# All eight PSUM banks from one table, re-planned step orders, and the late weight loads moved to another queue

## What is computed

```python
x = _layernorm(x + attn0(x))   # 16 heads of 8, low-rank q and k, causal softmax
x = _layernorm(x + ffn0(x))    # silu gate to 512, two 512x512 layers with gelu, down to 128
x = _layernorm(x + attn1(x))   # 16 heads of 8, softmax without a mask
x = _layernorm(x + ffn1(x))    # router picks 1 of 8 low-rank additions, relu, down to 128
```

## Time and profile before

| | us |
|---|---|
| median of three runs | 955.86 (951.77 to 958.83) |
| the profiled execution, its own time | 957.05 |
| its span, first to last instruction | 955.1 |
| PE busy | 887.5 (93%) |
| DVE busy | 673.9 (71%) |
| ACT busy | 487.8 (51%) |

### The profile page before, as it was taken

One profiled execution on the slowest core, in us unless ns is written; L12 is line 12 of the kernel. 1 busy time (PEld: TensorE's weight loads), 2 busy tenths in 40 slices (PEclk: granted clock), 3 DMA queues, 4 the chain that ended last, 5 costly groups with the idle time before them and its releaser, 6 DMA issues.

```text
span 955.1 us, 19245 instructions
## 1 busy us (share of the span) xinstructions
PE 887.5 (93%) x7076; PEld 690.3 (72%) x7076; DVE 673.9 (71%) x2379; ACT 487.8 (51%) x951; POOL 184.3 (19%) x389
## 2 busy tenths in 40 slices
PE   4598999999999999999999999999999999999995
PEld 3365887867667876678777887788767887778653
DVE  3867657759996569963698579956888659554843
ACT  0043654367455645644647365636555575563461
POOL 1032312003310233100420033101420123011011
PEclk9578999999998999989999999999999999999897
DMA  8514031402232024200243024120422022001200
GB/s 284 144 30 128 14 96 51 114 22 79 69 91 63 1 85 130 84 2 24 69 125 91 8 73 126 55 57 16 125 80 69 7 69 68 1 28 47 84 8 12
DMA packets 48900, 65.17 MB, mean 68 GB/s; under 512 B 5608, under 2 KB 42728, under 8 KB 44232
## 3 DMA queue, kind: packets, MB, share of 16 engines
q1 hardware_dynamic: 46840, 60.38, 21.8%
q10 hardware_dynamic: 1968, 3.57, 1.1%
HBM read 48.46 MB, written 14.68 MB: 66 GB/s over the span
## 4 chain that ended last, share of the span: by engine, by line
PE 47%; DVE 15%; issue 7%; DMA 4%; ACT 2%; SPq 2%; POOL 1%; POOLq 0%; DVEq 0%; ACTq 0%
PE ps_g L981 16%; PE ps_g L912 6%; PE ps_s L894 6%; DVE top L682 5%; PE ps_s L861 4%; PE ps_g L963 3%; PE ps_g L1030 3%; DMA krow<-scratch 2%; PE ps_g L816 1%; ACT prob L556 1%; PE ps_g L1011 1%; PE ps_g L1012 1%; DVE x L752 1%; DMA qrow<-tsplit 1%; PE ps_g L942 1%
## 5 line engine op out<-in xcount | busy, mean ns | idle before, releaser
L556 ACT ACTIVATE prob<-ps_s 128x384 f32<-128x384 f32 (+1 forms) x512 | 250.8, 552 | 111.3 <-PE ps_s L894 86.8
L682 DVE TENSOR_REDUCE top<-ps_s 128x2 f32<-128x512 f32 (+1 forms) x280 | 180.7, 683 | 46.3 <-PE ps_s L861 37.7
L673 DVE CUSTOM_DVE_ANT_0 ps_s<-ps_s,above 128x128 f32<-128x128 f32 x448 | 145.8, 386 | 30.0 <-PE ps_s L861 26.4
L894 PE MATMUL ps_s<-qrow,krow 75*128 75x256 bf16 (+1 forms) x1024 | 159.8, 266 | 7.2 <-DMA qrow<-tsplit 4.4
L861 PE MATMUL ps_s<-krow,qrow 72*128 72x256 bf16 x768 | 146.1, 281 | 13.2 <-DVE top L682 5.7
L493 POOL TENSOR_TENSOR ln_rstd<-ln_var,minus_half 128x2 f32<-128x2 f32 x64 | 45.0, 705 | 419.1 <-DVE ln_var L742 418.9
L894 PEld LDWEIGHTS ps_s<-qrow,krow 75*128 75x128 bf16 x1024 | 89.2, 100 | 47.8 <-ACT prob L556 18.9
L912 PE MATMUL ps_g<-prob,v 128*32 128x256 f32 (+1 forms) x2048 | 121.1, 363 | 1.8 <-DVE glu L763 0.7
L981 PE MATMUL ps_g<-glu,wh 128*128 128x256 f32 x512 | 120.8, 391 | 0.0
L981 PE MATMUL ps_g<-hid,wh 128*128 128x256 f32 x512 | 115.7, 380 | 0.0
L981 PEld LDWEIGHTS ps_g<-glu,wh 128*128 128x128 f32 x512 | 97.8, 196 | 14.7 <-issue 0.8
(11 more groups left out here) (99 smaller groups left out, 1171.6 us busy)
## 6 DMA issues: line engine op xcount, KB each, us to landing
qrow<-scratch SPq DMA_DIRECT2D x30, 576.0 KB
krow<-scratch SPq DMA_DIRECT2D x90, 192.0 KB
scratch<-split SPq DMA_DIRECT2D x96, 128.0 KB, 1.9
wh<-in_wh SPq DMA_DIRECT2D x1, 2048.0 KB, 11.5
xt<-in_xt SPq DMA_DIRECT2D x16, 128.0 KB, 2.4
x<-in_x SPq DMA_DIRECT2D x16, 128.0 KB, 2.3
out<-xout SPq DMA_DIRECT2D x16, 128.0 KB, 2.0
qrow<-tsplit SPq DMA_DIRECT2D x90, 8.0 KB
```

Of the source, the lines that this page charges most:

```text
L556: nc.scalar.activation(prob[s][:, j % 2, g, 0:wide], ps_s2[:, (GROUP * j + g) % PSUM2, 0:wide], ACT.Exp, scale=1.0 / float(np.sqrt(np.floa ...
L673: done = nc.vector.tensor_tensor_reduce(out=bank[:, g * wide:(g + 1) * wide], in0=bank[:, g * wide:(g + 1) * wide], in1=above[:, 2 * P - w ...
L682: nc.vector.tensor_reduce(out=dst, in_=src, axis=AX, op=ALU.max, negate=True).then_inc(maxed[s], 1)
L894: done = nc.tensor.matmul(bank[:, kb * SEQ:(kb + 1) * SEQ - q0], krow[s][n % DEEP[s]][0:ROWSM, h, kb * P:(kb + 1) * P], qrow[s][n % DEEP[s ...
```

## The change

Three things are changed together; what is computed, and each engine's set of steps, stays the same except for `late`.

1. One tensor `banks` of eight banks takes the place of the three. `BANK_TABLE` has a digit for each use, in PE's order, so `pass1` and `pass2` too now write whichever bank the table names, and wait for the last reader of that bank, whatever step and engine that was.
2. All five strings of `SEQUENCE` are new. The letters are assigned anew too, so they are not to be compared one by one.
3. Loads: `late` is gone from SP. ACT issues `wh` in two halves and then `w3`, behind the key rows of chunk 0. `wv` and `rows` go behind ACT's wait for the folding weights. DVE's scaling waits for each half by itself (`weights3`, `weights4`), and its four steps are spread: DVE's new order starts `abawcccccccdwcccccwfwcccc` (a `qk`, b `v`, w `scale`, c `pass1`, d `early`, f `maxima`). SP's starts `qqaqradrffarq` (q `load`, a the writes to scratch, r `fetch`, d and f the rows of maxima), where it was `yqaqrardeqearq` (the same with e for the rows of maxima). ACT's starts `aame` where it was `amaf` (m the key rows, the last letter the first `pass2`). PE's starts `abaccccccccdcccceeefeeeeeggcecccc` where it was `abaccccccccdccccecffcffcfcffcffcfg` (before: e `maxima`, f `pass2`; after: e `pass2`, f `maxima`).

```diff
-PSUM1, PSUM2 = 2, 3
-SHARED = 3
+BANKS8 = 8
+SHARED = BANKS8
...
-            of[step] = [(bank + i) % SHARED for i in range(count)]
+            of[step] = [int(b) for b in BANK_TABLE[bank:bank + count]]
...
-        ps_s1 = ps("ps_s1", [P, PSUM1, 512])
-        ps_s2 = ps("ps_s2", [P, PSUM2, 512])
-        ps_g = ps("ps_g", [P, SHARED, 512])
+        banks = ps("banks", [P, SHARED, 512])
...
-            def late(s, n):
-                sp.dma_start(wh[:], d_in["wh"]).then_inc(weights3, DMA)
-                sp.dma_start(w3raw, d_in["w3"]).then_inc(weights3, DMA)
...
+            nc.gpsimd.memset(top[A0][:].rearrange("p q h -> p (q h)"), 0.0)
             nc.gpsimd.memset(ident[:], 0.0)
...
+            act.wait_ge(weights0, 2 * DMA)
+            act.wait_ge(weights0b, DMA)
             act.dma_start(wv[A0][:], d_in["v_w0"]).then_inc(weights1, DMA)
             act.dma_start(rows[:], d_in["rows"].partition_broadcast(P)).then_inc(weights1, DMA)
-            act.wait_ge(weights0, 2 * DMA)
-            act.wait_ge(weights0b, DMA)
             act.dma_start(wo[A0][:], d_in["o_w0"]).then_inc(weights1, DMA)
...
+                for layer, there in enumerate((weights3, weights4)):     # at the end of key_rows
+                    act.dma_start(wh[:, layer], d_in["wh"][:, layer]).then_inc(there, DMA)
+                act.dma_start(w3raw, d_in["w3"]).then_inc(weights4, DMA)
...
                 elif k == 3:
+                    dve.wait_ge(weights4, 2 * DMA)
...
                     if k == 1:
-                        dve.wait_ge(weights3, NWEIGHTS3)
+                        dve.wait_ge(weights3, DMA)
+                    else:
+                        dve.wait_ge(weights4, 2 * DMA)
...
-            def pass1(s, n, j, u):
+            def pass1(s, n, j, u, b):
...
-                bank = ps_s1[:, k % PSUM1, :]
-                last.wait(pe, ("s1", k % PSUM1))
+                bank = banks[:, b, :]
+                last.wait(pe, b)
...
-            def pass2(s, n, j, g):
+            def pass2(s, n, j, g, b):
...
-                bank = ps_s2[:, (GROUP * j + g) % PSUM2, :]
-                last.wait(pe, ("s2", (GROUP * j + g) % PSUM2))
+                bank = banks[:, b, :]
+                last.wait(pe, b)
```

More of the change, by code:

```diff
@@ L68 @@
 CAUSAL = 2
-BARE = ('load', 'late', 'scale', 'keys', 'resid', 'fetch', 'pass1', 'pass2', 'norm', 'store')
+BARE = ('load', 'scale', 'keys', 'resid', 'fetch', 'norm', 'store')
 KIND = {
     "a": ("qk", A0), "b": ("v", A0), "c": ("pass1", A0), "d": ("early", A0),
-    "e": ("maxima", A0), "f": ("pass2", A0), "g": ("values", A0), "h": ("outputs", A0),
+    "e": ("pass2", A0), "f": ("maxima", A0), "g": ("values", A0), "h": ("outputs", A0),
     "i": ("merge", A0), "j": ("project", A0), "k": ("turn", A0), "l": ("norm", A0),
-    "m": ("keys", A0), "n": ("osum", A0), "o": ("causal", A0), "p": ("resid", A0),
+    "m": ("keys", A0), "n": ("osum", A0), "o": ("resid", A0), "p": ("causal", A0),
     "q": ("load", A0), "r": ("fetch", A0), "s": ("gated", F0), "t": ("hidden", F0),
     "u": ("down", F0), "v": ("turn", F0), "w": ("scale", F0), "x": ("norm", F0),
[L81 to L86, removed]
+    "y": ("qk", A1), "z": ("v", A1), "A": ("pass1", A1), "B": ("maxima", A1),
+    "C": ("pass2", A1), "D": ("values", A1), "E": ("outputs", A1), "F": ("merge", A1),
+    "G": ("project", A1), "H": ("turn", A1), "I": ("early", A1), "J": ("norm", A1),
+    "K": ("osum", A1), "L": ("resid", A1), "M": ("fetch", A1), "N": ("route", F1),
+    "O": ("lora", F1), "P": ("expert", F1), "Q": ("down", F1), "R": ("norm", F1),
+    "S": ("resid", F1), "T": ("store", F1),
 }
@@ L445, in store @@
                 sp.dma_start(out[bass.ts(n, TOK), :].rearrange("(t p) d -> p t d", p=P), x["out"][n % AHEAD][:]).then_inc(stored[n % AHEAD], DMA)
-            walk(dict(load=load, late=late, qk=park, fetch=fetch, maxima=maxima, early=early, store=store), "sp")
+            walk(dict(load=load, qk=park, fetch=fetch, maxima=maxima, early=early, store=store), "sp")
             for i in range(AHEAD):
@@ L815, in qk @@
                 for side in range(2):
-                    done = nc.tensor.matmul(ps_g[:, g, side * TOK:(side + 1) * TOK], wq[s][:, side, :], xt[s][n % AHEAD][:], start=True, stop=True)
+                    done = nc.tensor.matmul(banks[:, g, side * TOK:(side + 1) * TOK], wq[s][:, side, :], xt[s][n % AHEAD][:], start=True, stop=True)
                 done.then_inc(proj_full[s], 1)
```

175 lines of the change are left out of this document (96 added, 79 removed).

## The result

The changed kernel takes **925.63 us** (median of 4 runs, 920.99 to 927.51) against 957.35 (median of 4, 951.77 to 960.47) for the kernel before beside it: ratio **0.9668, 95% interval 0.9606 to 0.9730**. The prediction was 945, range 933 to 958. The sign was right (a gain that can be told had the largest chance, 0.50), the size was not: 32 us instead of 12, and outside the range. The profiled run took 927.51 us, its span is 925.7 us where it was 955.1.

What follows compares the result with a forecast made beforehand. The prediction took the kernel to be bound by PE's order, its work plus short waits. From 957.05 us it took 4.9 for the loads, 7.0 for the banks and 0 for the orders: 945 us, range 933 to 958.

Steps and rivals of the forecast that it cites:

- What bounds the kernel: Whole run: PE's order binds, its work plus short waits; busy PE, 93% of the span, hides gaps up to 0.16 us.
- Part 1, the start: Loads before the first pass1: 7.1 us earlier, less 2.2 for scalings, net 4.9 us faster; ends 0.1 and 9.
- fetch that shares with `wh`: Query-row fetch at the start: sharing engines with wh could delay the first pass1 by 2.5 us; in range, not sum.
- moved scalings: DVE's scalings of wh and w3, now between pass1 steps: 5.24 us in all, of which 2.2 us show.
- the tail: End of the last chunk: order nearly letter for letter the same, its 35 us with PE at 22.24 stay.
- Part 2, the banks: Score-bank waits on PE: about 0.3 of 30 us goes, 7 us stay as gain; ends 0 and 14.
- two DVE-heavy stretches: 240 to 300 and 360 to 420 us: DVE busy 51.6 and 55.3 of 60, so freed banks give nothing there.
- Part 3, the orders: New step orders on all engines: same work, reordering costed at 0, with ends of -4 and +6 us.
- Only the loads pay: Rival: bank waits go, but PE then waits for the same DVE or ACT step as data; 952 us, chance 0.27.
- Both in full: Rival: the start gives 7.1 us or more and the banks 14; 935 us, chance 0.17.
- The banks tie the engines together: Rival: shared banks make score steps wait for late readers of other kinds; 975 us at 60 more waits, chance 0.11.
- The clock: Rival: longer pass1 runs and pauses bring more PE clock drops, losing 11 us; 956 us, no change, chance 0.05.

Runs made afterwards that it cites:

- e1: The changed kernel with its loads undone (wh and w3 first on SP's queue, scalings ahead of pass1), new bank table and orders kept: 932.8 us, 0.9785 of the kernel before.
- e4: The kernel before, its orders and bank groups kept, with the new loads and the scalings spread on DVE: 956.3 us, 1.0011 of the kernel before.
- e7: The kernel before, its orders and loads, with eight shared banks in a table made from traced durations to follow the readers: 965.1 us, 1.0089 of the kernel before.
- e3: The kernel before, its orders and loads, with eight shared banks, each use taking the one used longest ago: 1082.3 us, 1.1351 of the kernel before.
- e8: The changed kernel with its bank table replaced by one made from traced durations to follow the readers: 938.5 us, 0.9813 of the kernel before.
- e10: The changed kernel with four idle pauses on PE, before the first pass1 of chunks 4, 6, 8 and 10: 951.7 us, 0.9984 of the kernel before.
- e11: The changed kernel with products of zeros on PE before the first pass1 of chunks 4, 6, 8 and 10: 943.7 us, 0.9905 of the kernel before.

## Why the prediction was wrong, point by point

**What bounds the kernel** was read rightly in the main: PE's order, work plus short waits. PE's busy time fell by 17 us with the same matmuls, but a part of that is the clock and not hidden gaps (Part 3 has the middle). One reading was wrong: I wrote that four or five tenths of the clock are gone in slices 2 to 4, one in the middle and the end. That holds for slice 2 alone; slices 3 and 4 read 7 and 8, the two in the middle 8 and 8, the end 8, 9 and 7.

**Part 1, the start.** Right to a microsecond: `qk` at 12.8 predicted and 13.02 measured, the first `pass1` at 27.5 and 28.29, no wait for `wh`, which landed 8.5 us after its issue. The 2.5 us for a fetch that shares with `wh`, 30.0, didn't come: from `qk` to the first `pass1` it takes 15.3 us, and 14.3 in e1, where `wh` isn't on its way then, so 0.9 at most is seen. The Trainium skill's rule on turns between queues (DMA: Bandwidth & Descriptors, on queues, rings and completion order) is neither shown nor refuted by that. The cost of the moved scalings was sized 2.2 us; the wait they made was 4.0, so that the net of 4.9 was 3.6 at the first maxima and 2.6 at chunk 3. DVE was fuller in the 15 us from the first `pass1` on, as I had said, 13.07 for 11.56, and PE emptier for it, 9.83 for 12.76.

**What the start is worth at the end** I took to be the same 4.9 us. It doesn't look like a constant: some 7 to 11 us in the new orders (e1), nothing that shows in the old ones (e4). In the traces 2 to 3 us of the first go with one fall of the clock that the changed kernel doesn't have; and the second's lead of 3 to 6 us goes in the tail, where its fall is 11 us longer. Why the fall comes at all in one and is so long in the other is open.

**Part 2, the banks, is the step that failed together with Part 3.** I took 7 us for shared banks in any order, on the ground that a bank wait that goes gives its time back. In the old orders a table that follows the readers loses 8 us and one by age 126 (e7, e3). In e7 the bank waits went, 49.8 to 24.4 us, more than I had hoped for, and the time didn't, because PE then waited for the maxima and their rows. The share that I took from reuse distances, 0.3 of the waits, happens to be near the fall of the waits (47.7 to some 30, 33 predicted), and has no cause in it, since the table with the best distances was the worst, and e8 has fewer such waits than the change (19.4) and takes longer. That the two DVE-heavy stretches "can't give their part" was wrong of the change as a whole: the lead grows most around them, by 14.8 us from 238 to 471. DVE's full stretches are not a limit when the order spreads its work: over the whole of these 233 us before, DVE is busy 170 (80.37 + 89.84).

**Part 3, the orders, costed at 0 with ends of -4 and +6,** holds the rest. From 238 to 881 us, 19.9 us: 6.5 are idle time of PE that is gone (17.5 to 11.0, from the stretches above). Three falls of the clock, from 287, 413 and 707 on, are gone too. At e10's 2.7 us for one of 7 us, and 1.2 for the third, of 3 us, they make an estimate of 6.6 (by the medians, 2.0 and 0.9, it is 4.9). Some 7 to 9 us are left within PE's busy time: up to 3.2 are the 24 matmuls that the marks leave out, and the others fit the gaps of up to 0.16 us that hide there, which no run shows by itself. The falls are not the orders' alone: the trace of e8, with the new orders and loads but my table, has two of them again,

```profile
289.00:296.00 7.00, 7.00 (x37) 4.73 (x38) 3.26 (x20) 3.83 (x8) 1.38 (x2) 0.53 0.55 143
719.00:722.00 3.00, 2.85 (x7) 2.35 (x8) 0.91 (x5) 0.78 (x2) 0.00 (x0) 0.50 0.77 202
```

and that of e4, with the old orders, lacks two. The tail gives 5.0 of idle time and 1.9 more. I had called the tail unchanged from the end of the strings, "nearly letter for letter the same". The strings of its last letters are, but the steps before them are not. Which of the new orders' moves pays how much was not tried. The reason I gave for the 0, that one can't see from strings which wait comes last, was a reason for wide ends, not for a narrow zero: the rows for wider ends were there. In the two stretches of the earlier trace rows PE idles 6.9 of 120 us and 0.06 of the clock is missing, 7.2 us: 14 us that a better order could give back, about what it did give from 238 to 471.

**The rivals.** *Only the loads pay* (952): refuted as to the loads, which alone pay nothing that shows (e4), while the change still pays 2.1% without them (e1). But what it said of the bank waits, that PE then waits a little later for the same engines' results, is what e7 shows. *Both in full* (935): nearest in size, for other reasons. *The banks tie the engines together* (975): a true mechanism, 7.6 and 13.5% with tables by age, but it depends on the table, and the change's own table keeps clear of it. *The clock* (956): a true mechanism with the sign turned round. I looked for falls that the change would add, and had in the earlier trace rows those that it could take away: in the changed kernel the clock is 1.00 from 130 to 880 us, and in its repeat from 130 to 870.

**From the rule to the trace.** The Trainium skill, TensorE: Matmul & The Clock Gate, on re-throttling, tells that waits between groups of matmuls halve the clock again and again. The pauses of e10 agree, four of four, and in e11, with work in the gap, there is no fall at the same places. But not each wait does it here, as the one of 1.46 us ahead of 472 shows.

## What to carry to other kernels

Cost an order and its buffers as one thing: here the new PE order deadlocks on the old groups of banks, the shared banks are worth nothing in the old order, and new orders, banks and loads together are worth 3%. A wait for a buffer that goes is a gain only if the data behind it are there: e7 halved the bank waits and took 1% longer. When PE is the bound, count in the trace the places where its clock has fallen and what it waited for just ahead of each: here one of 7 us was worth its idle time and 2 to 2.7 us more. Don't judge a table of buffers by the distance between uses, nor by its waits alone; measure it.

## What the runs showed of the hardware that was not expected

- **Falls came after short waits, not after every one, and they differ in length.** In the kernel before the clock was 0.50 from 287 us on, behind waits of 0.34 and 1.59 us, and from 413 on, behind three of 0.37 us and less; in the changed kernel a wait of 1.46 us ahead of 472 brought none. The falls last from 3 us (707 to 710, kernel before) over 7 (901 to 908, the same) to 18 (895 to 913, e4), the last two under about the same work.
- **The recorded clock is not to be trusted at the start.** In the changed kernel the `pass1` matmuls of 128 columns start 0.107 us apart at 28.3 us (28.48, 28.59, 28.70) and 0.057 at 35 us (34.88, 34.94, 35.00), so PE was at half its speed first, while the clock is recorded as 1.00 throughout:

```profile
28.00:34.00 6.00, 5.71 (x44) 5.10 (x45) 4.31 (x7) 0.00 (x0) 0.00 (x0) 1.00 1.01 368
```

  e4 has 1.00 recorded from 28 to 57 us, and at 35 us its matmuls start 0.107 us apart (34.80, 34.90, 35.01), as the kernel before's do at a recorded 0.50. The spacing of starts of one known shape is the surer reading.
- **x landed in 4.7 us** (the median of three issues) where no `wh` and `w3` stood ahead of it, and in 15.6 behind their 2.25 MB on its own queue.
